# Attention maxima over two PSUM banks at once, and seven of sixteen tiles of the scan's drive by TensorE

## The chip, the core and the metric

The kernel runs on one core of one Trainium2 chip. The metric is the device time of one execution in microseconds; the time of before is the median of three runs. Engines: PE is TensorE, DVE is VectorE, ACT is ScalarE, POOL is GpSimd, SP is the queue that issues the DMAs.

## What is computed

Eight residual steps on x of 2048 tokens by 128 channels: a Mamba block with its own feed-forward, a mixture of experts, causal attention, the experts again, a second Mamba block, a low-rank MLP, causal attention with a position bias, the MLP again. Everything is float32. The change touches the two scans and the two attentions:

```python
# scan, per channel d (256) and state n (16), over the tokens t
h[d,n] = exp(delta[t,d] * A[d,n]) * h[d,n] + delta[t,d] * u[t,d] * B[t,n]
y[t,d] = sum_n h[d,n] * C[t,n]
# attention, 16 heads of 8 channels, 2048 tokens, causal
dots = einsum("hid,hjd->hij", q, k) * scale    (+ bias in the second)
attn = softmax(where(j > i, -max, dots))
out  = einsum("hij,hjd->hid", attn, v)
```

## The kernel before

The kernel is written engine by engine: each engine has its own list of instructions, in the order of the code, and waits on semaphores. Nothing reorders them but the code. Eight stages follow each other.

**The scan** (`mamba_state`, at about 58 to 260 and 1196 to 1400 us of the trace). A step q handles one state number n for 1024 tokens (half k = q // 16 of the tokens), for both halves h = 0, 1 of the channels; there are 32 steps. For each h DVE scans `state = decay * state + drive` over 1024 columns (L596). The two drives, delta\*u\*B, are made in two ways. For h = 0, PE spreads the row of B over the partitions into PSUM (`rows`, L396, two matmuls of 512 columns) and DVE multiplies it by du in place (`make_drive`, L576, 1024 columns). For h = 1, PE makes the first four tiles of 128 tokens as products of the transposed du (`du_T`) with a diagonal of B's column (`products`, L407; the diagonals are made by ACT, L490), POOL multiplies the other 512 columns (`make_part`, L646) and ACT copies them into PSUM (L519). A product of 128 columns stands in the trace as two matmul records. After a scan POOL multiplies the state by C (`read`, L668) and PE adds that up (`sum_states`, L420, eight records of 512 columns a step). PE's order in step q is: rows(q+1), products(q+1), sum_states(q). `products(q)` waits until both scans of step q - 1 are done, `rows(q)` until the first of them is. At the stage's start du is made by four DVE multiplies (`times_u`, L566), the fourth after the first two scans.

**The attention** (`attention`, 524 to 957 and 1505 to 1927 us). For each head there are two passes over the causal half. In the first, PE makes query by key dots into `ps_q` and DVE finds each query's maximum. It goes over 40 *items* a head, numbered n = 0 to 39: an item is one tile t of 128 queries against one chunk kc of 512 keys (`q_items`; t = 0 to 3 have one chunk, t = 12 to 15 have four). An item is a group of four matmuls of 32 columns of the array each (`item`, L1679), which run beside each other. DVE reads its bank in one operation: L1861 for a full chunk, L1858 with the mask for the last one (of 128 to 512 columns, followed by a read of the accumulator). `ps_q` has QB = 3 banks, used in turn; the item that takes use number `use` waits for `bank_free(use)`:

```python
def bank_free(use):
    if use >= QB:
        pe.wait_ge(q_read, use - QB + 1)
```

When a head's 40 maxima are found (L1866), POOL splits them into three bf16 parts, PE turns them (`turn`, L1663, also into a bank of `ps_q`, at position TURN = 5 of the next head's items), DVE casts them (L1849) and SP stores them as three more rows of `q_op`. The second pass makes key by query scores with the maximum already subtracted into `ps_k` (`scores`, L1693, and L1697 for the mask), ACT takes the exp (L1797), and PE multiplies by v (`times_v`, L1715) into `ps_o`, of two banks; ACT copies a finished chunk of 512 queries out (L1805).

PE interleaves both passes. The second pass of a head runs beside the first pass of the next. A *slot* is one scores group and then one item group; after each fourth slot comes one `times_v` of four chunks. Items run LEAD = 14 positions ahead of a head's worth, so the slots of a head's second pass begin with item 14 of the next head, and a `times_v` stands right behind items 1, 5, 9, 13, ... 37:

```python
for a in range(n, n + 4):
    b = NK * h + a
    if b + KB < NK * HEADS:
        scores(b + KB)
    stream(turn, item, NQ + LEAD + b, NQ + LEAD + b + 1)
times_v(h, n)
```

## Time and profile before

| what | us |
|---|---|
| median of 3 runs | 1998.84 |
| lowest, highest | 1994.96, 2001.33 |
| the profiled execution | 1991.66 |
| its span, first to last instruction | 1989.9 |
| PE, DVE, ACT, POOL busy in the span | 1802.1, 1585.1, 1176.7, 592.4 |
| both attentions' second passes (first to last exp) | 400, 399 |
| both scans (first drive to last read) | 201, 201 |

The busy time of an engine is the union of its instructions. For PE it is flattering: the ends of matmuls are modelled, and a group of four overlaps with the next, so starts say more than durations. DVE's and ACT's durations overlap with the next instruction too: what an operation costs its engine is the distance between two starts. "Idle before <-X" names what the engine waited for last.

### The profile page before, as it was taken

The numbers are of one execution on the slowest core, as the hardware profiler recorded it, in microseconds if no ns is written. First come the engines' busy times: TensorE is split into PE (matmuls) and PEld (weight loads), VectorE is DVE, ScalarE is ACT, GpSimd is POOL, SyncE is SP. The second block draws the span as 40 slices with busy tenths as digits, with TensorE's granted clock in tenths as the row PEclk, the third lists the DMA queues.
The fourth block names the chain that finished last, engine by engine and source line by source line (L and its number), as shares of the span: only waits on it lengthen the run. The fifth ranks groups of instructions, "written<-read, shape, count | busy, mean of one in ns | idle before, by whom it ended". The sixth has DMA issues, their size and how long they took to land. (4 is left out here: it accounts for less than half of the span.)

```text
span 1989.9 us, 48041 instructions
## 1 busy us (share of the span) xinstructions
PE 1802.1 (91%) x18610; PEld 961.7 (48%) x18610; DVE 1585.1 (80%) x3424; ACT 1176.7 (59%) x2363; POOL 592.4 (30%) x556
## 2 busy tenths in 40 slices
PE   6888888999799999999899978888888999999988
PEld 2444454444355555555444434444543555555544
DVE  6899966666789999996556678999668999999855
ACT  4676623222268888887422257766352888888855
POOL 3899931000200000004000038999430000000142
PEclk9999998999789999999999998999996999999998
DMA  5433400311312222222041113343012222232200
GB/s 160 121 129 127 128 11 0 86 49 37 106 30 51 51 51 51 51 40 40 1 86 48 37 56 116 133 125 124 1 42 83 49 55 55 56 55 55 31 23 22
DMA packets 68801, 127.94 MB, mean 64 GB/s; under 512 B 20343, under 2 KB 30853, under 8 KB 67165
## 3 DMA queue, kind: packets, MB, share of 16 engines
q1 hardware_dynamic: 68284, 124.34, 24.3%
q8 instruction: 147, 2.41, 0.5%
q14 instruction: 82, 0.66, 0.1%
q10 hardware_dynamic: 288, 0.52, 0.1%
HBM read 107.15 MB, written 16.48 MB: 62 GB/s over the span
## 5 line engine op out<-in xcount | busy, mean ns | idle before, releaser
L1797 ACT ACTIVATE a_probs<-a_ps_k 128x512 f32<-128x512 f32 (+3 forms) x1280 | 599.6, 545 | 216.5 <-PE a_ps_k L1697 135.2
L1861 DVE TENSOR_REDUCE a_maxes<-a_ps_q 128x1 f32<-128x512 f32 x768 | 504.1, 685 | 66.9 <-PE a_ps_q L1679 64.2
L1679 PE MATMUL a_ps_q<-a_k_op,a_q_op 84*32 84x512 bf16 (+7 forms) x5120 | 536.3, 366 | 23.2 <-DMA a_k_op<-a_k_parts 8.7
L1693 PE MATMUL a_ps_k<-a_q_op,a_k_op 87*32 87x512 bf16 (+7 forms) x5120 | 513.0, 351 | 4.0 <-ACT a_probs L1797 3.4
L1715 PE MATMUL a_ps_o<-a_probs,a_vh 128*32 128x512 f32 (+3 forms) x2752 | 316.1, 505 | 0.8 <-ACT a_probs L1797 0.8
L1679 PEld LDWEIGHTS a_ps_q<-a_k_op,a_q_op 72*32 72x32 bf16 (+1 forms) x5120 | 187.1, 97 | 169.7 <-DVE a_maxes L1861 68.8
L1858 DVE CUSTOM_DVE_ANT_0 a_ps_q<-a_ps_q,all_c_mask_q 128x128 f32<-128x128 f32 (+3 forms) x512 | 248.1, 495 | 4.0 <-PE a_ps_q L1679 3.0
L1693 PEld LDWEIGHTS a_ps_k<-a_q_op,a_k_op 75*32 75x32 bf16 (+1 forms) x5120 | 184.1, 96 | 131.7 <-ACT a_probs L1797 78.6
L1113 ACT ACTIVATE e_silu<-e_psg,all_me_b 128x512 f32<-128x512 f32 x128 | 87.7, 687 | 228.1 <-PE e_psg L1045 228.1
L1942 POOL CAST a_max_parts<-a_neg_max 128x16 bf16<-128x16 f32 x32 | 6.3, 196 | 705.3 <-DVE a_neg_max L1866 705.3
L1196 DVE SCALAR_TENSOR_TENSOR e_mid<-e_psv,all_me_b,e_silu 128x512 f32<-128x512 f32 x128 | 95.6, 748 | 129.1 <-PE e_psv L1047 125.2
L172 POOL TENSOR_TENSOR all_rstd<-all_var_eps,all_c_minus_half 128x4 f32<-128x4 f32 x36 | 36.8, 1022 | 467.0 <-DVE all_var_eps L161 466.9
L668 POOL TENSOR_TENSOR m1st_read<-m1st_state,m1st_c_rows 128x1024 f32<-128x1024 f32 x64 | 149.6, 2358 | 11.2 <-PE m1st_psy L420 7.9
L596 DVE TENSOR_TENSOR_SCAN m1st_state<-m1st_decay,m1st_carry,m1st_drive 128x1024 f32<-128x1024 f32 x64 | 146.8, 2334 | 7.6 <-DVE m1st_drive L576 6.4
L668 POOL TENSOR_TENSOR m0st_read<-m0st_state,m0st_c_rows 128x1024 f32<-128x1024 f32 x64 | 149.6, 2359 | 10.7 <-DVE m0st_state L596 6.4
L596 DVE TENSOR_TENSOR_SCAN m0st_state<-m0st_decay,m0st_carry,m0st_drive 128x1024 f32<-128x1024 f32 x64 | 146.8, 2334 | 7.6 <-DVE m0st_drive L576 6.4
L1697 PE MATMUL a_ps_k<-all_c_mask_k,all_c_ident_b 128*32 128x128 bf16 x2048 | 148.5, 221 | 1.1 <-issue 0.9
L1045 PE MATMUL e_psg<-e_xT,all_me_w_T 128*128 128x512 f32 x256 | 133.9, 605 | 1.5 <-ACT e_xT L197 1.5
L1047 PE MATMUL e_psv<-e_xT,all_me_w_T 128*128 128x512 f32 x256 | 132.3, 599 | 0.0
L1034 PE MATMUL e_pso<-e_hid,all_me_w_T 128*128 128x512 f32 x256 | 119.6, 596 | 4.5 <-DVE e_hid L1205 4.5
L1715 PEld LDWEIGHTS a_ps_o<-a_probs,a_vh 128*32 128x32 f32 x2752 | 106.7, 110 | 26.2 <-ACT a_probs L1797 1.1
L420 PE MATMUL m1st_psy<-m1st_read,all_c_ident 128*128 128x512 f32 x256 | 116.1, 594 | 2.0 <-POOL m1st_read L668 1.8
(294 smaller groups left out, 2585.2 us busy)
## 6 DMA issues: line engine op xcount, KB each, us to landing
...
```

The source lines that it names most:

```text
L596: dve.tensor_tensor_scan(state[half(q, h)][:, :], decay[half(q, h)][:, :], drive[:, h, :], carry[:, h, q % NS:q % NS + 1], ALU.mult, ALU.a ...
L668: pool.tensor_tensor(read[h][:, :], state[half(q, h)][:, :], c_rows[q % 2][:, :], ALU.mult).then_inc(read_ready, 1)
L1034: pe.matmul(pso[:, :], w["w3_T"][:, e, f, :], hid[:, k % SL, :], start=k == 0, stop=k == K - 1, skip_group_check=True).then_inc(hid_free, 1)
L1045: pe.matmul(psg[:, f, :], w["w1_T"][:, e, fs], xT[:, tokens(c)], start=True, stop=True).then_inc(g_ready, 1)
L1047: pe.matmul(psv[:, f, :], w["w2_T"][:, e, fs], xT[:, tokens(c)], start=True, stop=True).then_inc(v_ready, 1)
L1679: last = pe.matmul(ps_q[32 * r:32 * r + 32, use % QB, 0:width], q_op[h % SLOT][0:NR, part(t, r)], k_op[h % SLOT][0:NR, kc * CH:kc * CH + w ...
L1693: last = pe.matmul(ps_k[32 * r:32 * r + 32, b % KB, 0:width], k_op[h % SLOT][:, part(j, r)], q_op[h % SLOT][:, c * CH + first:c * CH + fir ...
L1697: last = pe.matmul(ps_k[32 * r:32 * r + 32, b % KB, 0:P], g["ident_b"][:, part(0, r)], g["mask_k"][:, :], start=False, stop=True, skip_gro ...
L1715: pe.matmul(ps_o[rows, c % 2, lo:hi], vh[h % SLOT][:, j, :], probs[:, a % PSLOT, lo - first:hi - first], start=j < 4, stop=j >= TPC * c, s ...
L1797: act.activation(probs[:, n % PSLOT, 0:width], ps_k[:, b % KB, 0:width], ACT.Exp).then_inc(exp_done, 1)
L1858: dve.tensor_tensor_reduce(bank, bank, g["mask_q"][:, CH - width:CH], 1.0, -3e38, ALU.add, ALU.max, found).then_inc(q_read, 1)
L1861: dve.tensor_reduce(found, bank, AX.X, ALU.max).then_inc(q_read, 1)
```

## The change

In the scan, the drive of h = 1 has five tiles made by PE (DIAGONALS = 5) and 384 columns by POOL, and the drive of h = 0 has its first two tiles made by PE (FIRST = 2, `first_products`, with the same diagonals and two more tiles of `du_T`) and 768 columns by DVE. ACT makes five diagonals a step, and its copy into PSUM waits for the fifth tile, which lies in the same bank (`late_made`). Two pieces of the start move: the turn of B's columns stands after four more matmuls on PE, and the fourth `times_u` on DVE before the first scan.

In the attention, the two chunks kc = 0, 1 and the two chunks kc = 2, 3 of a query tile are one *find*: PE fills two neighbouring banks, DVE takes one maximum over up to 1024 columns. There are 24 finds a head, of which 16 take two items: (4, 5), (6, 7), (8, 9), (10, 11), then (12, 13), 14, (15, 16), 17, (18, 19), 20, (21, 22), 23, and (24, 25), (26, 27) and so on to (38, 39). `ps_q` has QB = 2 such double banks, four banks in all, and the bank for that comes from `ps_o`, which has one now. The turn stands at position 6.

```diff
-                for j in range(TPC):
+                for j in reversed(range(DIAGONALS)):
                     last = pe.matmul(drive[:, 1, tile(j)], du_T[:, q // NS, j, :], diag_b[q % 2][:, j, :], start=True, stop=True)
+                    if j == TPC:
+                        last.then_inc(late_made, 1)
...
+            def first_products(q):
+                pe.wait_ge(diag_ready, q + 1)
+                if q % NS == 0:
+                    pe.wait_ge(du_copied, q // NS + 1)
+                if q:
+                    pe.wait_ge(scanned, NH2 * (q - 1) + 1)
+                for j in range(FIRST):
+                    last = pe.matmul(drive[:, 0, tile(j)], du_T[:, q // NS, DIAGONALS + j, :], diag_b[q % 2][:, j, :],
+                                     start=True, stop=True)
+                last.then_inc(first_made, 1)
...
                 if q and q + 1 < STEPS:
+                    first_products(q + 1)
                     rows(q + 1)
                     products(q + 1)
...
-                dve.tensor_tensor(drive[:, 0, :], du[:, 0, time(q)], drive[:, 0, :], ALU.mult).then_inc(drive_ready, 1)
+                dve.tensor_tensor(drive[:, 0, FIRST * P:SCT], du[:, 0, time(q, FIRST * P)], drive[:, 0, FIRST * P:SCT], ALU.mult).then_inc(drive_ready, 1)
...
-        QB = 3
+        QB = 2
         LEAD = 14
-        TURN = 5
+        TURN = 6
...
-        ps_q = m.ps("ps_q", [P, QB, CH])
+        ps_q = m.ps("ps_q", [P, QB, 2 * CH])
-        ps_o = m.ps("ps_o", [P, 2, CH])
+        ps_o = m.ps("ps_o", [P, CH])
...
-                bank_free(use)
+                if n == find_begins[f]:
+                    bank_free(use)
                 for r in range(4):
-                    last = pe.matmul(ps_q[32 * r:32 * r + 32, use % QB, 0:width], q_op[h % SLOT][0:NR, part(t, r)],
+                    last = pe.matmul(ps_q[32 * r:32 * r + 32, use % QB, at:at + width], q_op[h % SLOT][0:NR, part(t, r)],
                                      k_op[h % SLOT][0:NR, kc * CH:kc * CH + width], start=True, stop=True,
                                      skip_group_check=True)
-                last.then_inc(q_ready, 1)
+                if n == find_ends[f]:
+                    last.then_inc(q_ready, 1)
...
-                if n in begins and NC * h + c >= 2:
-                    pe.wait_ge(o_read, NC * h + c - 1)
+                if n in begins and NC * h + c:
+                    pe.wait_ge(o_read, NC * h + c)
...
+                if n != find_ends[f]:
+                    return
+                t, kcs = finds[f]
+                width = min(2 * CH, (t + 1) * P - kcs[0] * CH)
                 dve.wait_ge(q_ready, use + 1)
```

PE's instructions in the first attention from item 19 to item 21, before. Names in brackets are semaphores that the instruction waits for; a semaphore keeps the name of its first holder in the program, and here number 158 is `q_read` and 175 is `exp_done`.

```order
L1679 MATMUL a_ps_q<-a_k_op_274,a_q_op_273 32x512 [waits m0st_summed_158]
L1679 MATMUL a_ps_q<-a_k_op_274,a_q_op_273 32x512 x3
L1693 MATMUL a_ps_k<-a_q_op_271,a_k_op_272 32x384 [waits m0o_t_ready_175]
L1693 MATMUL a_ps_k<-a_q_op_271,a_k_op_272 32x384 x3
L1697 MATMUL a_ps_k<-all_c_mask_k,all_c_ident_b 32x128 x4
L1679 MATMUL a_ps_q<-a_k_op_274,a_q_op_273 32x384 [waits m0st_summed_158]
L1679 MATMUL a_ps_q<-a_k_op_274,a_q_op_273 32x384 x3
L1693 MATMUL a_ps_k<-a_q_op_271,a_k_op_272 32x256 [waits m0o_t_ready_175]
L1693 MATMUL a_ps_k<-a_q_op_271,a_k_op_272 32x256 x3
L1697 MATMUL a_ps_k<-all_c_mask_k,all_c_ident_b 32x128 x4
L1679 MATMUL a_ps_q<-a_k_op_274,a_q_op_273 32x512 [waits m0st_summed_158]
L1679 MATMUL a_ps_q<-a_k_op_274,a_q_op_273 32x512 x3
```

The same place after:

```order
L1715 MATMUL a_ps_q<-a_k_op_276,a_q_op_275 32x512 x4
L1730 MATMUL a_ps_k<-a_q_op_273,a_k_op_274 32x384 [waits m0o_o_read_175]
L1730 MATMUL a_ps_k<-a_q_op_273,a_k_op_274 32x384 x3
L1734 MATMUL a_ps_k<-all_c_mask_k,all_c_ident_b 32x128 x4
L1715 MATMUL a_ps_q<-a_k_op_276,a_q_op_275 32x384 [waits m0st_carried_158]
L1715 MATMUL a_ps_q<-a_k_op_276,a_q_op_275 32x384 x3
L1730 MATMUL a_ps_k<-a_q_op_273,a_k_op_274 32x256 [waits m0o_o_read_175]
L1730 MATMUL a_ps_k<-a_q_op_273,a_k_op_274 32x256 x3
L1734 MATMUL a_ps_k<-all_c_mask_k,all_c_ident_b 32x128 x4
L1715 MATMUL a_ps_q<-a_k_op_276,a_q_op_275 32x512 [waits m0st_carried_158]
L1715 MATMUL a_ps_q<-a_k_op_276,a_q_op_275 32x512 x3
```

Items 19, 20 and 21 and the scores between them stand in the same order; item 19 no longer waits, and item 21's wait is now for the double bank of items 18 and 19.

PE in the scan, one step, before (m0st_read is summed up, then the next step's rows and products):

```order
L407 MATMUL m0st_drive<-m0st_diag_b_106,m_du_T 128x128 x4
L420 MATMUL m0st_psy<-m0st_read_100,all_c_ident 128x512 x2
L420 MATMUL m0st_psy<-m0st_read_101,all_c_ident 128x512 x2
L396 MATMUL m0st_drive<-m_bc_82,all_c_sel 128x512 x2
L407 MATMUL m0st_drive<-m0st_diag_b_107,m_du_T 128x128 x4
```

and after:

```order
L440 MATMUL m0st_psy<-m0st_read_100,all_c_ident 128x512 x2
L440 MATMUL m0st_psy<-m0st_read_101,all_c_ident 128x512 x2
L417 MATMUL m0st_drive<-m0st_diag_b_107,m_du_T 128x128 x2
L406 MATMUL m0st_drive<-m_bc_82,all_c_sel 128x256
L406 MATMUL m0st_drive<-m_bc_82,all_c_sel 128x512
L425 MATMUL m0st_drive<-m0st_diag_b_107,m_du_T 128x128 x5
L440 MATMUL m0st_psy<-m0st_read_100,all_c_ident 128x512 x2
```

Two products now stand ahead of the rows, and the rows that DVE waits for are behind them.

DVE at the first stage's start, from around the copy of B's columns to behind the first two scans, before:

```order
L607 COPY m_b_cols<-m0stin_turned 128x320
L566 TENSOR_TENSOR m_du<-m_delta,m_u 128x2x512 x2
L570 COPY m_du_T<-m0stin_acc 128x512
L576 TENSOR_TENSOR m0st_drive<-m_du,m0st_drive 128x1024
L566 TENSOR_TENSOR m_du<-m_delta,m_u 128x2x512
L596 SCALAR_TENSOR_TENSOR m0st_state_105<-m0st_decay_98,m0st_carry,m0st_drive 128x1024
L596 SCALAR_TENSOR_TENSOR m0st_state_102<-m0st_decay_99,m0st_carry,m0st_drive 128x1024
L570 COPY m_du_T<-m0stin_acc 128x512
L566 TENSOR_TENSOR m_du<-m_delta,m_u 128x2x512
```

and after:

```order
L592 TENSOR_TENSOR m_du<-m_delta,m_u 128x2x512
L636 COPY m_b_cols<-m0stin_turned 128x400
L592 TENSOR_TENSOR m_du<-m_delta,m_u 128x2x512
L597 COPY m_du_T<-m0stin_acc 128x896
L604 TENSOR_TENSOR m0st_drive<-m_du,m0st_drive 128x768
L592 TENSOR_TENSOR m_du<-m_delta,m_u 128x2x512 x2
L624 SCALAR_TENSOR_TENSOR m0st_state_105<-m0st_decay_98,m0st_carry,m0st_drive 128x1024
L624 SCALAR_TENSOR_TENSOR m0st_state_102<-m0st_decay_99,m0st_carry,m0st_drive 128x1024
L597 COPY m_du_T<-m0stin_acc 128x896
```

The fourth multiply into m_du has moved ahead of both scans, and the copies of du_T are 896 columns wide.

## Rows read from the trace of the kernel before

**Rows 1.** Busy time by stretches of 80 us (scan) and 300 us (attention): us, engines, PEclk
```profile
75.00:155.00 80.00, 67.47 (x246) 34.46 (x247) 77.18 (x42) 56.81 (x124) 79.96 (x42) 1.00 0.38 129
...
600.00:900.00 300.00, 296.87 (x5820) 173.87 (x5818) 275.61 (x717) 248.34 (x541) 13.47 (x65) 1.00 0.27 49
```

**Rows 2.** Timeline of DVE in the attention: start us, us, engine, line, operation
```profile
676.43 0.14 DVE L1858 DVE_READ_ACCUMULATOR2_ANT a_maxes<- 128x1 f32 x1
...
677.03 0.27 DVE L1849 CAST a_max_T<-a_ps_q 48x128 bf16<-48x128 f32 x1
...
678.22 0.69 DVE L1861 TENSOR_REDUCE a_maxes<-a_ps_q 128x1 f32<-128x512 f32 x1 [0.65 <-PE a_ps_q L1679]
...
701.43 0.27 DVE L1849 CAST a_max_T<-a_ps_q 48x128 bf16<-48x128 f32 x1
```

**Rows 3.** Timeline of PE, same stretch: turn of the maxima, items around it
```profile
672.95 0.41 PE L1679 MATMUL a_ps_q<-a_k_op,a_q_op 72*32 72x512 bf16 x4
...
673.70 0.29 PE L1679 MATMUL a_ps_q<-a_k_op,a_q_op 72*32 72x256 bf16 x4
...
676.16 0.24 PE L1663 MATMUL a_ps_q<-all_c_ident_b,a_max_parts 128*32 128x128 bf16 x2
...
676.63 0.24 PE L1679 MATMUL a_ps_q<-a_k_op,a_q_op 72*32 72x128 bf16 x4 [0.23 <-DVE a_maxes L1858]
...
677.77 0.39 PE L1679 MATMUL a_ps_q<-a_k_op,a_q_op 72*32 72x512 bf16 x4
...
680.35 0.39 PE L1693 MATMUL a_ps_k<-a_q_op,a_k_op 75*32 75x512 bf16 x4
```

**Rows 4.** Timeline of PE, one head earlier: items 13 to 24
```profile
657.07 0.39 PE L1679 MATMUL a_ps_q<-a_k_op,a_q_op 72*32 72x512 bf16 x4
...
658.17 0.54 PE L1679 MATMUL a_ps_q<-a_k_op,a_q_op 72*32 72x512 bf16 x4
...
660.73 0.38 PE L1679 MATMUL a_ps_q<-a_k_op,a_q_op 72*32 72x512 bf16 x1
...
661.58 0.40 PE L1679 MATMUL a_ps_q<-a_k_op,a_q_op 72*32 72x512 bf16 x3
...
662.79 0.39 PE L1679 MATMUL a_ps_q<-a_k_op,a_q_op 72*32 72x512 bf16 x3
...
663.66 0.45 PE L1679 MATMUL a_ps_q<-a_k_op,a_q_op 72*32 72x512 bf16 x4
```

**Rows 5.** Timeline of DVE in the attention: maxima back to back
```profile
706.19 1.28 DVE L1861 TENSOR_REDUCE a_maxes<-a_ps_q 128x1 f32<-128x512 f32 x2
...
707.39 0.29 DVE L1858 CUSTOM_DVE_ANT_0 a_ps_q<-a_ps_q,all_c_mask_q 128x128 f32<-128x128 f32 x1
...
707.60 1.28 DVE L1861 TENSOR_REDUCE a_maxes<-a_ps_q 128x1 f32<-128x512 f32 x2
```

**Rows 6.** Timeline of the scan, one step: DVE, then PE
```profile
185.93 1.20 DVE L576 TENSOR_TENSOR m0st_drive<-m_du,m0st_drive 128x1024 f32<-128x1024 f32 x1
...
187.34 4.58 DVE L596 TENSOR_TENSOR_SCAN m0st_state<-m0st_decay,m0st_carry,m0st_drive 128x1024 f32<-128x1024 f32 x2 [0.20 <-DVE m0st_drive L576]
...
191.84 1.21 DVE L576 TENSOR_TENSOR m0st_drive<-m_du,m0st_drive 128x1024 f32<-128x1024 f32 x1
...
186.16 1.13 PE L407 MATMUL m0st_drive<-m0st_diag_b,m_du_T 128*128 128x128 f32 x8 [0.91 <-DVE m0st_state L596]
...
187.13 3.60 PE L420 MATMUL m0st_psy<-m0st_read,all_c_ident 128*128 128x512 f32 x8
...
190.56 0.60 PE L396 MATMUL m0st_drive<-m_bc,all_c_sel 96*128 96x512 bf16 x2
```

**Rows 7.** DMA issues: operands, count, size, us to landing
```profile
a_q_parts<-a0pr_q_parts SPq DMA_DIRECT2D x12, 128.0 KB, 2.5
```

**Rows 8.** Groups by line: ACT's copy of the outputs
```profile
L1805 ACT ACTIVATE a_o_sb<-a_ps_o 128x512 f32<-128x512 f32 x128 | 75.9, 593 | 2.2 <-PE a_ps_o L1715 2.2
```

**Rows 9.** Timeline of DVE at the first scan's start
```profile
66.68 3.02 DVE L566 TENSOR_TENSOR m_du<-m_delta,m_u 128x1024 f32<-128x1024 f32 x1
```

More of the change, by code:

```diff
@@ L41 @@
 NSC = TOK // SCT
+DIAGONALS = 5
+FIRST = 2
+MADE = DIAGONALS * P
+LATE = SCT - MADE
 FF = 512
@@ L250, in mamba_state @@
         state.insert(0, m.sb("state0", [P, SCT]))
-        diag_b = [m.sb(f"diag_b{s}", [P, TPC, P]) for s in range(2)]
+        diag_b = [m.sb(f"diag_b{s}", [P, DIAGONALS, P]) for s in range(2)]
         carry = m.sb("carry", [P, NH2, NS])
@@ L333, in early_chunk @@
             return k * SCT // CH
+        turned_tiles = [(1, j) for j in range(DIAGONALS)] + [(0, j) for j in range(FIRST)]
         def time(q, first=0, last=SCT):
@@ L347, in turn_b @@
                 for k in range(NSC):
[L348 to L350 removed]
+                    pe.wait_ge(xd_ready, early_chunk(k) + 2)
+                    for j in range(DIAGONALS):
+                        at = (DIAGONALS * k + j) * XDBL
                         last = pe.transpose(turned[:, 1, at:at + XDBL], xd[0:XDBL, tile(TPC * early_chunk(k) + j)], g["ident"][0:XDBL, 0:XDBL])
@@ L395, in rows @@
                 for b in range(NB):
-                    last = pe.matmul(drive[:, 0, chunk(b)], g["sel"][:, q % NS, :], bc3[:, time(q, b * CH, (b + 1) * CH)],
+                    lo, hi = max(b * CH, FIRST * P), (b + 1) * CH
+                    last = pe.matmul(drive[:, 0, lo:hi], g["sel"][:, q % NS, :], bc3[:, time(q, lo, hi)],
                                      start=True, stop=True)
                 last.then_inc(rows_spread, 1)
-            def products(q):
+            def first_products(q):
                 pe.wait_ge(diag_ready, q + 1)
@@ L488, in diagonals @@
                     act.wait_ge(product_ready, q - 1)
-                for j in range(TPC):
+                for j in range(DIAGONALS):
                     last = act.activation(diag_b[q % 2][:, j, :], g["ident"][:, :], ACT.Identity,
@@ L516, in _ @@
                 act.wait_ge(part_ready, q + 1)
+                act.wait_ge(late_made, q + 1)
+                if q == 0:
+                    act.wait_ge(du_copied, 1)
                 if q:
                     act.wait_ge(scanned, NH2 * q)
-                act.activation(drive[:, 1, MADE:SCT], part[q % 2][:, :], ACT.Copy).then_inc(part_placed, 1)
+                act.activation(drive[:, 1, MADE:SCT], part[q % 2][:, 0:LATE], ACT.Copy).then_inc(part_placed, 1)
                 carry_over(q - 1, 1)
@@ L614, in _ @@
             times_u(2)
+            times_u(3)
             scans(0)
             copy_turned(1)
-            times_u(3)
             for q in range(1, STEPS):
@@ L645, in make_part @@
                     pool.wait_ge(part_placed, q - 1)
-                pool.tensor_tensor(part[q % 2][:, :], du[:, 1, time(q, MADE)], b_rows[q % 2][:, :],
+                pool.tensor_tensor(part[q % 2][:, 0:LATE], du[:, 1, time(q, MADE)], b_rows[q % 2][:, 0:LATE],
                                    ALU.mult).then_inc(part_ready, 1)
@@ L1588, in attention @@
         NQ = len(q_items)
+        finds = [(t, tuple(kc for kc in range(t // TPC + 1) if kc // 2 == half)) for t in range(NT) for half in range(t // TPC // 2 + 1)]
+        find_of = [f for f, (t, kcs) in enumerate(finds) for kc in kcs]
+        find_begins = [find_of.index(f) for f in range(len(finds))]
+        find_ends = [b - 1 for b in find_begins[1:]] + [NQ - 1]
         q_begins = [min(i for i, (t, kc) in enumerate(q_items) if t // TPC == c) for c in range(NC)]
@@ L1712, in times_v @@
                     if c == 0 and j:
-                        pe.matmul(ps_o[rows, 0, 0:first], zeros[:, :], g["sel"][:, 0:j, :], start=True, stop=True,
+                        pe.matmul(ps_o[rows, 0:first], zeros[:, :], g["sel"][:, 0:j, :], start=True, stop=True,
                                   skip_group_check=True)
-                    pe.matmul(ps_o[rows, c % 2, lo:hi], vh[h % SLOT][:, j, :], probs[:, a % PSLOT, lo - first:hi - first],
+                    pe.matmul(ps_o[rows, lo:hi], vh[h % SLOT][:, j, :], probs[:, a % PSLOT, lo - first:hi - first],
                               start=j < 4, stop=j >= TPC * c, skip_group_check=True).then_inc(pv_done, 1)
```

103 lines of the change are left out of this document (56 added, 47 removed).

## Prediction

> **What bounds the kernel now.** I read the busy table by stretches first. In the attentions PE is busy 296.9 of 300 us, DVE 275.6, ACT 248.3, at full clock; in the scan POOL is busy 80.0 of 80 us, DVE 77.2, PE 67.5 [rows 1]. The two casts of the maxima one head apart, 677.03 and 701.43, give the attention's beat, 24.40 us a head [rows 2]. Then the timeline of PE alone: item groups (four 32-column matmuls of 512 columns) and scores groups follow each other every 0.22 us: from item 22 at 662.79 to item 24 at 663.66 stand four of them in 0.87 us [rows 4], and 512 columns at 2.4 GHz are 0.213. So PE streams nearly without a gap, and whatever stops it is added to the head. The one long stop is at the turning of the maxima: turn at 676.16, next item at 676.63, 0.47 us for a group worth 0.06, "idle 0.23 <-DVE" [rows 3]. By the starts below DVE has maxima for 21 us of the 24.4, and waits for PE in between. **PE is the bound of the attentions, DVE is not, though it is close.**
>
> In the scan DVE sets the step: drive at 185.93, scans at 187.34, next drive at 191.84, so 5.91 us, with no wait but 0.20 us for its own result. PE ends its last rows matmuls (190.56 + 0.60) at 191.16, 0.68 us before DVE wants them [rows 6].
>
> **The attention's part.** It removes 16 of 40 DVE operations a head. From starts, a 512-column maximum costs 0.60 us (two from 706.19 to 707.39) and a 128-column one 0.21 (707.39 to 707.60) [rows 5], so 0.13 us for each 128 columns and some 0.07 fixed: DVE saves 16 x 0.07 = 1.1 us a head, worth nothing while PE is the bound. What is left is the buffering. Before, an item group needed the bank of three uses ago; now a group that begins a find needs the double bank of two finds ago, and both groups of that find must have been read in one operation. That takes, from the start of the find's last group: 0.45 us until DVE starts (group 677.77, DVE 678.22 [rows 2, 3]); 0.69 us for a 512-column maximum [rows 5] plus 512 more columns at 1.04 ns, together 1.22; and 0.06 us until PE's next matmul (the read of the accumulator ends at 676.57, PE starts 676.63 [rows 2, 3]). **1.73 us.** Each beginning find has that only if the eight products with v (0.86 us) stand between, since two slots (a scores and an item group each) without them are 0.87 us [rows 4]. Going through the 24 finds of a head in the order of the code with LEAD = 14, where a product block follows items 1, 5, 9, ... 37:
> - Item 1 needs find (38, 39). 672.95 to 673.70 is 0.75 [rows 3]: stop 0.98.
> - Item 4 needs item 2's bank, of 384 columns: the groups between them are 1920 columns, 0.82 us at 0.22 for 512; the read needs 0.39 + 0.61 + 0.06 = 1.06: 0.24.
> - Item 15 needs find (12, 13). 657.07 to 658.17 is 1.10 [rows 4]: 0.63, plus up to 0.3 as DVE still reads the 1024 columns before it, whose two slots gave it 0.87 for 1.14. I take 0.8.
> - Item 18 needs find (15, 16): a product block of uneven pieces stands between, 0 to 0.5. I take 0.1, since item 15's stop has already spread them.
> - Item 21 needs find (18, 19). The last group of 19 starts at 660.73, item 21 at 661.58, 0.85: 0.88.
> - Item 24 needs find (21, 22). 662.79 to 663.66, 0.87: 0.86 to 0.93; I take 0.9.
> - All others have a product block or a short find between them: no stop.
>
> Sum 3.9 us. The stop at the turn, 0.41, goes: the turn now stands behind a product block. But it comes a slot and a block later: the distance from it to the next head's first scores, 676.16 to 680.35, 4.2 us, shrinks to 2.6 (from 677.77 [rows 3]), and the maxima need about 0.3 to DVE, 0.27 for the cast [rows 2], and 2.5 to land (the nearest is the landing of the q parts, larger but to the same side [rows 7]): 3.1, a stop of 0.5, between 0 and 1; I take 0.3. Net 3.9 - 0.4 + 0.3 = **3.8 us a head**, 28.2 for 24.4. It applies to items 54 to 640 of each attention, 14.65 heads, 29.3 in both: **+110 us**. Bounds: half of the stops hidden in PE's short queues gives 2.8 a head, +82; every bound at its top, 4.7, +138. The first head, items alone, I put at nothing (DVE bound, 1.1 less, against a refill that now waits longer). Removing an output buffer (ps_o) puts times_v of a new chunk behind ACT's copy of the last one, 0.59 us, before which ACT waited for PE 2.2 us in 128 copies [rows 8]. The copy follows the exp that the block waits for anyway, so PE can be stopped 0 to 0.5 us four times a head; since PE, stopped by the finds, will be behind ACT, I take 0.
>
> DVE shows the stop's other side: the 1024 columns cost it a fixed 0.07 less. The Trainium skill, Perfetto Trace Analysis, section Optimizing Scalar/DVE Operations, says both that grouping into larger operations helps "if the engine is saturated", and that where Vector is not saturated but causes bubbles elsewhere, breaking instructions up lets work complete sooner. By the first DVE would be the bound and the change gain; by the second it loses. Rows 1 and 3 put this kernel in the second case.
>
> **The scan's part.** DVE's drive goes from 1024 to 768 columns, 256 x 1.04 ns = 0.27 us less a step; POOL's part from 512 to 384, a quarter of a job that is 1.28 with its fixed cost, so about as much. The step would be 5.64. PE pays: three more products at 0.243 (four took 186.16 to 187.13) less 256 columns of rows, 0.11 [rows 6]. Its chain from the end of the scans: products at +0.23 after the drive's start, then 5 x 0.243 + 3.43 (187.13 to 190.56) + 2 x 0.243 + 0.11 + 0.38 and 0.04 to DVE = 5.88. In a step where the scans end first PE is late by 0.24; in the next PE had no wait and only 5.65 is asked. The two alternate: 5.76, **0.15 us less a step**, 29 steps, two stages: -9. Bounds: 0.03 and 0.27 a step, -2 and -16. At the start of each stage DVE's fourth times_u took 3.02 us [rows 9] where the same 1024 columns of drive take 1.20: it ran beside POOL's read. It moves ahead of the first scan, where POOL waits: up to 1.8 gained, against wider copies (three tiles, 0.4 us each) and a fifth diagonal: I take -1 a stage, 1 either way. **-11 in all.** In a sentence apart: the Trainium skill, SBUF — State Buffer, section Who interferes with whom, says a tensor_tensor with both inputs in SBUF contends with GpSimd's reads; the 3.02 us agree.
>
> **Sum.** 1991.7 (profiled run, 1989.9 of it span) + 110 - 11 = 2091. The median shown, 1998.8, is 7.2 above the profiled run, so **2098**.
>
> **Rivals.**
> - *As meant: no stop.* PE's queues and DVE's lead cover the reuse. Then the turn's 0.41 goes, 29.3 x 0.4 = 12 us, and the scan's 11: 1999 - 23 = 1976. For it: DVE gets 1.1 us a head more room. Against: it decides at 1.73 us between a find's last group and its reuse, and four places give 0.75 to 1.1. If DVE were the bound after all, 1.1 x 29.3 = 32 more, 1944. Chance 0.10 together.
> - *Half of it.* The stops overlap with waits that PE has anyway (ACT's, the turn's): 1.5 to 2.5 a head, 2035 to 2060. For it: a stopped PE meets ACT further ahead, so that the short waits it has for ACT now go. Chance 0.08.
> - *More than it.* The single output buffer stops PE 0.3 us four times a head, 35 us more, or the clock falls. Against the clock: the scan keeps 1.00 with PE busy 84% [rows 1], and the attention would be at 85%. 2133 to 2170, chance 0.08.
> - *The scan alone differs*: -2 to -18, inside the range. That it gains nothing and the attention too: within 0.3%, 0.02.
>
> **How the numbers follow.** The forecast has 0.72, from 2062 (2.8 a head, scan -18) to 2135 (4.7 a head, scan -2). The range 2040 to 2140 takes in most of the half case and the low end of the one with more, and leaves out 0.19. Faster by over 0.3% (about what a measurement of this kernel can tell from no change) 0.10, within 0.02, slower 0.88.
>
> **What would show it.** In the profile after: the casts of the maxima about 28.2 us apart instead of 24.40; PE's idle before items naming DVE, near 1 us each, at items 1, 15, 21 and 24; busy PE some 85% in the attention; maxima over 1024 columns at 1.14 us from start to start (were it 1.5, every stop grows by 0.35). In the scan, steps of 5.64 and 5.88 in turn, and DVE's drive waiting for PE's rows. Wrong if the casts stay within 25 us of each other: then the reuse distance is not what the groups' starts say.

## The result

| | before | after |
|---|---|---|
| median, us | 1996.9 (1994.77 to 2001.33) | 2117.32 (2114.72 to 2120.89) |
| ratio | 1 | 1.0597, 95% interval 1.0573 to 1.0621 |
| profiled execution, its span | 1991.66, 1989.9 | 2114.72, 2112.9 |

The kernel became 6% slower. The forecast was 2098, in a range of 2040 to 2140; the loss is 120 us where 99 were forecast. The gap between the two profiled spans, 123.0 us, divides as follows. The times are differences between rows of the traces: a scan stage from the end of its last copy into xd to its last read, a first head from the first item to the first exp, the later heads from the first exp to the last.

| stretch, us | before | after | difference | forecast |
|---|---|---|---|---|
| scans | 208.3, 209.1 | 210.1, 210.1 | +2.8 | -11 |
| first heads of the attentions | 32.1, 32.0 | 37.4, 36.8 | +10.1 | 0 |
| other heads | 400.4, 399.7 | 454.0, 455.0 | +108.9 | +110 |
| the rest | 708.2 | 709.5 | +1.3 | 0 |

(The last column was worked out ahead of the result for other stretches' ends, so it is right to about 1 us.)

**The attention's heads.** The casts of the maxima, on DVE after the change:

```profile
701.04 0.28 DVE L1886 CAST a_max_T<-a_ps_q 48x128 bf16<-48x128 f32 x1 [0.23 <-PE a_ps_q L1696]
...
729.23 0.28 DVE L1886 CAST a_max_T<-a_ps_q 48x128 bf16<-48x128 f32 x1 [0.23 <-PE a_ps_q L1696]
...
757.44 0.28 DVE L1886 CAST a_max_T<-a_ps_q 48x128 bf16<-48x128 f32 x1 [0.23 <-PE a_ps_q L1696]
```

They stand 28.19 and 28.21 us apart, where it was 24.40 [rows 2]. PE over one head after the change; the columns are start, us, engine, line, operation, tiles, and in brackets the idle time before it with what ended it:

```profile
677.63 0.40 PE L1730 MATMUL a_ps_k<-a_q_op,a_k_op 75*32 75x512 bf16 x4
678.63 0.40 PE L1715 MATMUL a_ps_q<-a_k_op,a_q_op 72*32 72x512 bf16 x4 [0.60 <-DVE a_maxes L1901]
...
682.02 0.23 PE L1734 MATMUL a_ps_k<-all_c_mask_k,all_c_ident_b 128*32 128x128 bf16 x4
683.02 0.40 PE L1715 MATMUL a_ps_q<-a_k_op,a_q_op 72*32 72x512 bf16 x4 [0.77 <-DVE a_maxes L1901]
...
684.88 0.39 PE L1730 MATMUL a_ps_k<-a_q_op,a_k_op 75*32 75x512 bf16 x4
685.95 0.40 PE L1715 MATMUL a_ps_q<-a_k_op,a_q_op 72*32 72x512 bf16 x4 [0.68 <-DVE a_maxes L1901]
...
695.63 0.40 PE L1730 MATMUL a_ps_k<-a_q_op,a_k_op 75*32 75x512 bf16 x4
696.92 0.29 PE L1715 MATMUL a_ps_q<-a_k_op,a_q_op 72*32 72x256 bf16 x4 [0.89 <-DVE a_maxes L1898]
...
698.72 0.41 PE L1730 MATMUL a_ps_k<-a_q_op,a_k_op 75*32 75x512 bf16 x4
699.20 0.40 PE L1715 MATMUL a_ps_q<-a_k_op,a_q_op 72*32 72x512 bf16 x4
...
700.78 0.22 PE L1696 MATMUL a_ps_q<-all_c_ident_b,a_max_parts 128*32 128x128 bf16 x2
700.87 0.40 PE L1715 MATMUL a_ps_q<-a_k_op,a_q_op 72*32 72x512 bf16 x4
...
703.24 0.39 PE L1715 MATMUL a_ps_q<-a_k_op,a_q_op 72*32 72x512 bf16 x4
703.65 0.40 PE L1730 MATMUL a_ps_k<-a_q_op,a_k_op 75*32 75x512 bf16 x4
```

These are the stops of the prediction, in its places. The group after a 512-column group should start 0.22 us later. Item 15 starts 1.00 after its predecessor (677.63 to 678.63), so it stops 0.78; item 21 stands 1.00 behind a mask group worth 0.06, a stop of 0.94; item 24 1.07 behind a group worth 0.22, so 0.85; item 1 (256 columns, 696.92) 1.29, so 1.07; item 4 (699.20) 0.48 behind a group worth 0.22, so 0.26, though no bracket stands there. The turn at 700.78 is followed by an item at 700.87: its stop is gone. The first scores of the next head, at 703.65, come 0.41 behind an item of 512 columns: 0.19 for the landing of the maxima.

There is a sixth stop, at item 18, which the prediction gave 0.1. No bracket shows it, since PE still had pieces of the product block at work. PE at items 16 to 19 and DVE's read of items 15 and 16, after the change:

```profile
679.07 0.39 PE L1715 MATMUL a_ps_q<-a_k_op,a_q_op 72*32 72x512 bf16 x4
...
679.51 0.28 PE L1715 MATMUL a_ps_q<-a_k_op,a_q_op 72*32 72x256 bf16 x4
...
680.79 0.40 PE L1715 MATMUL a_ps_q<-a_k_op,a_q_op 72*32 72x512 bf16 x4
...
681.30 0.39 PE L1715 MATMUL a_ps_q<-a_k_op,a_q_op 72*32 72x512 bf16 x4
```

```profile
679.51 1.23 DVE L1901 TENSOR_REDUCE a_maxes<-a_ps_q 128x1 f32<-128x1024 f32 x1 [0.68 <-PE a_ps_q L1715]
```

and items 17 and 19 before:

```profile
659.19 0.29 PE L1679 MATMUL a_ps_q<-a_k_op,a_q_op 72*32 72x256 bf16 x4
...
660.49 0.38 PE L1679 MATMUL a_ps_q<-a_k_op,a_q_op 72*32 72x512 bf16 x1
```

Item 18 starts at 680.79, 1.72 us after item 16's group (679.07) and 0.05 after the end of the read (679.51 + 1.23 = 680.74): the same chain as in the other places. From item 17 to item 19 it is 1.79 us where it was 1.30, so 0.49 more. Item 21, in turn, had stood late before the change too: from item 19 to item 21 it is 1.72 us where it was 1.09 (660.49 to 661.58 [rows 4]), 0.63 more and not 0.94. With 0.49 at item 18 and 0.63 at item 21, and 1.07, 0.26, 0.78 and 0.85 in the other places, 0.19 for the landing and 0.41 less at the turn, the head is 3.86 us longer by this count; 3.79 were measured.

DVE shows the price of one long read:

```profile
684.67 1.22 DVE L1901 TENSOR_REDUCE a_maxes<-a_ps_q 128x1 f32<-128x1024 f32 x1 [1.17 <-PE a_ps_q L1715]
685.81 0.69 DVE L1898 CUSTOM_DVE_ANT_0 a_ps_q<-a_ps_q,all_c_mask_q 128x512 f32<-128x512 f32 x1
```

From 684.67 to 685.81, 1.14 us for 1024 columns, as in the prediction's working. DVE did save its 16 operations, and stands idle for them: over the same 300 us as in [rows 1] the row is

```profile
600.00:900.00 300.00, 268.01 (x5060) 135.31 (x5056) 238.26 (x450) 220.99 (x470) 11.41 (x55) 1.00 0.24 43
```

PE is busy 268.0 us of 300 where it was 296.9, DVE 238.3 where it was 275.6. The clock is 1.00 in this stretch in both kernels, with PE idle for 0.60 to 0.89 us four times in each 28 us after the change. Nothing of the loss in these heads is clock.

**The scan.** DVE and then PE in two steps after the change:

```profile
188.48 0.96 DVE L604 TENSOR_TENSOR m0st_drive<-m_du,m0st_drive 128x768 f32<-128x768 f32 x1
...
194.14 0.94 DVE L604 TENSOR_TENSOR m0st_drive<-m_du,m0st_drive 128x768 f32<-128x768 f32 x1
...
199.98 0.96 DVE L604 TENSOR_TENSOR m0st_drive<-m_du,m0st_drive 128x768 f32<-128x768 f32 x1
...
188.43 1.38 PE L425 MATMUL m0st_drive<-m0st_diag_b,m_du_T 128*128 128x128 f32 x10
...
193.53 0.49 PE L406 MATMUL m0st_drive<-m_bc,all_c_sel 96*128 96x256 bf16 x2
194.29 1.38 PE L425 MATMUL m0st_drive<-m0st_diag_b,m_du_T 128*128 128x128 f32 x10 [0.27 <-DVE m0st_state L624]
```

The drives start at 188.48, 194.14 and 199.98: steps of 5.66 and 5.84 in turn, where it was 5.91 [rows 6]. The mean is 0.16 less. Yet the stage gains nothing, because its opening costs more. PE and ACT at the first drive, after the change:

```profile
56.10 1.28 ACT L523 ACT_TABLE_LOAD   x1
57.40 1.15 ACT L523 ACTIVATE m0st_decay<-m_delta,m_neg_a 128x1024 f32<-128x1024 f32 x1
58.45 1.55 ACT L513 ACTIVATE m0st_diag_b<-all_c_ident,m_b_cols 128x128 f32<-128x128 f32 x5
...
60.06 1.23 PE L417 MATMUL m0st_drive<-m0st_diag_b,m_du_T 128*128 128x128 f32 x4 [3.46 <-ACT m0st_diag_b L513]
...
69.29 2.50 PE L425 MATMUL m0st_drive<-m0st_diag_b,m_du_T 128*128 128x128 f32 x10 [0.31 <-DVE m0st_state L624]
```

The first drive (DVE, 61.52) waits for the two products of `first_products`, these for ACT's diagonals, and ACT makes those only after loading its table and the first decay. From the end of the last copy into xd to the first drive it is 11.75 us where it was 6.76. TensorE's clock falls 8 to 10 us after that copy in both kernels. After the change it stays at 0.50 for 13.5 us; before, it did for 3.3 us in the first scan and for 10.1 in the second. The rows, after and then before, have the stretch, its length, the busy us and records of PE, of its weight loads, of DVE, ACT and POOL, the granted clock, the DMA share and GB/s:

```profile
59.50:73.00 13.50, 10.66 (x39) 8.50 (x40) 11.35 (x8) 8.63 (x20) 5.65 (x3) 0.50 0.02 5
```

```profile
61.50:64.80 3.30, 3.27 (x14) 2.81 (x14) 2.27 (x2) 3.30 (x7) 2.09 (x2) 0.50 0.11 29
1198.10:1208.20 10.10, 7.40 (x25) 5.42 (x26) 9.07 (x6) 9.37 (x21) 7.31 (x4) 0.50 0.10 33
```

At 0.50 TensorE runs at its lower level, 1.2 GHz: the ten product records took 2.50 us at 69.29, and 1.38 at 188.43. The scan of before varies along with this: its second to third drive takes 5.85 us in the first scan and 6.97 in the second, and over the six kernels that keep this scan (before, att_alone, one_output_bank, four_banks, reads_apart, lead_15) a stage takes 208.1 to 210.1 us, 209.4 in the mean. So the +2.8 of the table is exact for the two traces only; against the mean it is +1.4. Both are far from the -11 that was forecast.

### The profile page after: what moved, and what is told of

Same layout as the page of the kernel before. It is cut to its first block and busy times, and to the rows that moved or that the text cites. A ratio compares the mean times of both kernels' runs of the same rounds, so it can differ in the third digit from the quotient of the medians.

```text
span 2112.9 us, 48465 instructions
## 1 busy us (share of the span) xinstructions
PE 1874.9 (89%) x19010; PEld 970.0 (46%) x19010; DVE 1563.6 (74%) x2912; ACT 1197.1 (57%) x2427; POOL 572.9 (27%) x556
## 5 line engine op out<-in xcount | busy, mean ns | idle before, releaser
L1834 ACT ACTIVATE a_probs<-a_ps_k 128x512 f32<-128x512 f32 (+3 forms) x1280 | 611.7, 539 | 321.7 <-PE a_ps_k L1734 202.1
L1715 PE MATMUL a_ps_q<-a_k_op,a_q_op 84*32 84x512 bf16 (+7 forms) x5120 | 500.5, 368 | 115.5 <-DVE a_maxes L1901 73.3
L1730 PE MATMUL a_ps_k<-a_q_op,a_k_op 87*32 87x512 bf16 (+7 forms) x5120 | 500.6, 352 | 4.0 <-ACT a_probs L1834 2.3
L1898 DVE CUSTOM_DVE_ANT_0 a_ps_q<-a_ps_q,all_c_mask_q 128x128 f32<-128x128 f32 (+7 forms) x512 | 385.8, 769 | 91.6 <-PE a_ps_q L1715 82.0
L1901 DVE TENSOR_REDUCE a_maxes<-a_ps_q 128x1 f32<-128x1024 f32 x256 | 313.0, 1223 | 93.5 <-PE a_ps_q L1715 93.2
L1715 PEld LDWEIGHTS a_ps_q<-a_k_op,a_q_op 72*32 72x32 bf16 (+1 forms) x5120 | 151.3, 98 | 304.8 <-DVE a_maxes L1901 127.4
L1730 PEld LDWEIGHTS a_ps_k<-a_q_op,a_k_op 75*32 75x32 bf16 (+1 forms) x5120 | 166.1, 96 | 123.8 <-ACT a_probs L1834 63.1
L176 POOL TENSOR_TENSOR all_rstd<-all_var_eps,all_c_minus_half 128x4 f32<-128x4 f32 x36 | 36.8, 1023 | 469.9 <-DVE all_var_eps L165 469.8
L696 POOL TENSOR_TENSOR m0st_read<-m0st_state,m0st_c_rows 128x1024 f32<-128x1024 f32 x64 | 149.5, 2357 | 21.9 <-DVE m0st_state L624 12.4
L1734 PE MATMUL a_ps_k<-all_c_mask_k,all_c_ident_b 128*32 128x128 bf16 x2048 | 128.2, 221 | 0.0
L1752 PEld LDWEIGHTS a_ps_o<-a_probs,a_vh 128*32 128x32 f32 x2752 | 98.3, 110 | 53.0 <-ACT a_o_sb L1842 12.6
```

The lines of the kernel that those rows point to most:

```text
L696: pool.tensor_tensor(read[h][:, :], state[half(q, h)][:, :], c_rows[q % 2][:, :], ALU.mult).then_inc(read_ready, 1)
L1715: last = pe.matmul(ps_q[32 * r:32 * r + 32, use % QB, at:at + width], q_op[h % SLOT][0:NR, part(t, r)], k_op[h % SLOT][0:NR, kc * CH:kc * ...
L1730: last = pe.matmul(ps_k[32 * r:32 * r + 32, b % KB, 0:width], k_op[h % SLOT][:, part(j, r)], q_op[h % SLOT][:, c * CH + first:c * CH + fir ...
L1734: last = pe.matmul(ps_k[32 * r:32 * r + 32, b % KB, 0:P], g["ident_b"][:, part(0, r)], g["mask_k"][:, :], start=False, stop=True, skip_gro ...
L1752: pe.matmul(ps_o[rows, lo:hi], vh[h % SLOT][:, j, :], probs[:, a % PSLOT, lo - first:hi - first], start=j < 4, stop=j >= TPC * c, skip_gro ...
L1834: act.activation(probs[:, n % PSLOT, 0:width], ps_k[:, b % KB, 0:width], ACT.Exp).then_inc(exp_done, 1)
```

## The experiments

All are timed against the kernel before on the same chip. reads_apart, lead_15, five_alone and first_alone were run once each, so there is a trace and a single time for them.

### att_alone: the attention's change on the scan of before

Against the kernel after, all of the scan's change is undone:

```diff
-DIAGONALS = 5
-FIRST = 2
...
                 if q and q + 1 < STEPS:
-                    first_products(q + 1)
                     rows(q + 1)
```

> The attention's change alone, on the scan of before. My theory (PE waits for a double bank to be read, 3.8 us a head): casts of the maxima 28.2 us apart, first head of each attention 4 to 5 longer too, so 110 + 9 = 119 us more than before, within 3 of the whole change. Rival (the scan's part carries some of the loss, since the scan's 31 steps in all show none of the 11 us forecast): 105 to 112 more than before.

Measured: 2116.56 against 1997.47, ratio 1.0594 (1.0565 to 1.0623). Casts 28.2 apart, first heads 37.6 and 37.2 us, the other heads 454.2 and 455.2. The attention carries the whole loss, +119; the rival falls.

### one_output_bank: before, with one bank less for ps_o

```diff
-        ps_o = m.ps("ps_o", [P, 2, CH])
+        ps_o = m.ps("ps_o", [P, CH])
...
-                if n in begins and NC * h + c >= 2:
-                    pe.wait_ge(o_read, NC * h + c - 1)
+                if n in begins and NC * h + c:
+                    pe.wait_ge(o_read, NC * h + c)
```

> Before, with one bank for the output of the second pass (ps_o) instead of two; one bank of PSUM stays unused. My theory, in which ACT's copy of the output stops PE for nothing: casts still 24.4 apart, within 3 us of before. Rival (part of the 3.8 us a head is the single output bank): up to 4 x 0.3 us a head, 35 us more.

Measured: 2001.01 against 1997.47, ratio 1.0013 (0.9988 to 1.0037), no difference that can be measured. The trace has it finer: most casts are 24.46 apart, 0.06 a head more than before, which is 2 us in all. Single heads take up to 1.7 us more in this trace (26.07, 25.57 and 25.55), as one does in the trace of before (25.51). With them the later heads of both attentions are 8.2 us longer in this trace; the interval of the times ends at 7.4 us more. So the bank that was taken from the output costs between nothing and some 8 us, and the rival's 35 fall.

### four_banks: the same banks, not paired

Against the kernel before, with one_output_bank's edit of `times_v` besides:

```diff
-        QB = 3
+        QB = 4
         LEAD = 14
         TURN = 5
...
-        ps_q = m.ps("ps_q", [P, QB, CH])
         with ExitStack() as early:
             turned = Memory(nc, early, tag + "pr").ps("turned", [P, 2, CH])
-        ps_o = m.ps("ps_o", [P, 2, CH])
+        ps_q = m.ps("ps_q", [P, QB, CH])
+        ps_o = m.ps("ps_o", [P, CH])
```

> The same four banks for the maxima and one for the output as after the change, but each item has a bank of its own, read and released alone, as before (QB = 4, TURN = 5). My theory: the bank was not the cost, the pairing was. No stop at items 1, 15, 21, 24, and the turn's 0.41 us stop goes too, since the item behind it has a spare bank: casts 23.9 to 24.0 apart, 12 to 16 us less than before. Rival (the order, the output bank or the turn costs): 26 or more.

Measured: 1986.98 against 1997.47, ratio 0.9946 (0.9930 to 0.9962): 10.5 us less, a little short of the 12 to 16 that were expected. Casts of its DVE:

```profile
703.63 0.27 DVE L1849 CAST a_max_T<-a_ps_q 48x128 bf16<-48x128 f32 x1
727.65 0.27 DVE L1849 CAST a_max_T<-a_ps_q 48x128 bf16<-48x128 f32 x1
```

24.02 us, 0.38 less than before: the turn's stop of 0.41 is gone, and nothing has come. PE's items as a group, in the page's form (line, engine, operation, tiles and count, busy us and mean ns, idle us before them with what ended it), in this kernel, before and after the change:

```profile
L1679 PE MATMUL a_ps_q<-a_k_op,a_q_op 84*32 84x512 bf16 (+7 forms) x5120 | 551.4, 365 | 15.4 <-DMA a_k_op<-a_k_parts 10.9 <-issue 1.6 <-DVE a_maxes L1858 1.3
```

```profile
L1679 PE MATMUL a_ps_q<-a_k_op,a_q_op 84*32 84x512 bf16 (+7 forms) x5120 | 536.3, 366 | 23.2 <-DMA a_k_op<-a_k_parts 8.7 <-DVE a_maxes L1858 8.4 <-DVE a_maxes L1861 3.2
```

```profile
L1715 PE MATMUL a_ps_q<-a_k_op,a_q_op 84*32 84x512 bf16 (+7 forms) x5120 | 500.5, 368 | 115.5 <-DVE a_maxes L1901 73.3 <-DVE a_maxes L1898 33.3 <-DMA a_k_op<-a_k_parts 6.2
```

With four single banks PE's idle time before items that is put down to DVE is 1.3 us for the masked reads and less than that for the others, in both attentions together (8.4 and 3.2 with three banks); with the same four banks read and released in pairs it is 73.3 and 33.3 us. The loss is the pairing's.

### reads_apart: double banks, read half by half

Against att_alone:

```diff
-                if n == find_ends[f]:
-                    last.then_inc(q_ready, 1)
+                last.then_inc(q_ready, 1)
...
-                if n != find_ends[f]:
-                    return
...
-                width = min(2 * CH, (t + 1) * P - kcs[0] * CH)
+                width = min(CH, (t + 1) * P - kc * CH)
```

(A double bank is released by the count of its second half; `bank_free` waits for that.)

> Double banks as after the change, released as a pair, but DVE reads each half as soon as its group is in: from the last group to the release only 0.45 + 0.69 + 0.06 = 1.20 us instead of 1.73. My theory: stops of about 0.45 (item 1), 0.24 (item 4), 0.1 to 0.3 (item 15), 0.35 (item 21) and 0.33 (item 24), the turn as after: casts 25.4 to 26.2 apart, although DVE has the 16 operations back. Rival (the length of the chain does not matter, only the number of double banks): 28.2.

Measured: 2058.77 in one run, casts 26.3 apart (719.27 and 745.58), 1.9 more than before and 1.9 less than after. The stops follow the length of the chain, 0.53 us shorter. It is a little more than the upper end expected. Two of its stops on PE:

```profile
794.00 0.29 PE L1691 MATMUL a_ps_q<-a_k_op,a_q_op 72*32 72x256 bf16 x4 [0.53 <-DVE a_maxes L1872]
...
807.27 0.40 PE L1691 MATMUL a_ps_q<-a_k_op,a_q_op 72*32 72x512 bf16 x4 [0.35 <-DVE a_maxes L1875]
```

The one at 794.00 is item 1, 0.53 by the bracket where it was 0.89, the one at 807.27 item 21, 0.35 where it was 0.77: 0.36 and 0.42 less, not the whole 0.53. At item 21 DVE's row shows why: it reads the two halves in one row, and the second can't start before the first is done.

```profile
805.93 1.29 DVE L1875 TENSOR_REDUCE a_maxes<-a_ps_q 128x1 f32<-128x512 f32 x2 [0.38 <-PE a_ps_q L1691]
```

It ends at 807.22, and item 21 starts 0.05 later: 1.55 us after item 19's group (805.72 in the trace) and not 1.20.

### lead_15: the product blocks one item later

Against att_alone:

```diff
-        LEAD = 14
+        LEAD = 15
```

> att_alone with LEAD = 15, so that the product blocks stand behind items 2, 6, 10, ... 38 and not 1, 5, 9, ... 37. My theory (a stop is 1.73 us less what stands between a double bank's last group and its reuse): the count over the finds gives stops at items 1, 2, 6, 10, 14, 15, 18, 21, 34 and 38, some 5.3 us for 4.2, and none for the landing of the maxima: casts 28.9 to 29.6 apart. Rival (the stop does not depend on where the blocks stand): 28.2, or less by the landing that is gone.

Measured: 2158.68 in one run, casts 29.68 apart, 1.5 more than in att_alone and just above the range. One number, that changes no work at all, costs 42 us: it puts product blocks where the finds don't need them. Six of its stops in a head have a bracket; these are the three at items 38, 6 and 14, that have no stop with LEAD = 14 (the others are 1, 18 and 21; all six are on the list of what was expected):

```profile
700.93 0.40 PE L1687 MATMUL a_ps_q<-a_k_op,a_q_op 72*32 72x512 bf16 x4 [0.17 <-DVE a_maxes L1870]
...
707.78 0.40 PE L1687 MATMUL a_ps_q<-a_k_op,a_q_op 72*32 72x512 bf16 x4 [0.52 <-DVE a_maxes L1870]
...
713.49 0.24 PE L1687 MATMUL a_ps_q<-a_k_op,a_q_op 72*32 72x128 bf16 x4 [0.29 <-DVE a_maxes L1870]
```

### scan_alone: the scan's change on the attention of before

Against the kernel after, all of the attention's change is undone:

```diff
-        QB = 2
+        QB = 3
...
-                if n == find_ends[f]:
-                    last.then_inc(q_ready, 1)
+                last.then_inc(q_ready, 1)
```

> The scan's change alone, on the attention of before. The trace of the whole change has steps of 5.66 and 5.83 us in turn (before 5.91), but from the last chunk's copy (xd) to the last drive of a stage it needs 1.0 and 1.8 us more than before. My theory: the opening of each stage loses 5 to 6 us (the first drive waits for ACT's diagonals, TensorE's clock stays at 0.50 from 60 to 72 us), the steps give 4.4 back: 0 to 3 us more than before. Rival (the opening differs only by run, my forecast of -11 holds): 8 to 14 less.

Measured: 1996.55 against 1997.5, ratio 1.0009 (0.9991 to 1.0028): no difference. The forecast of 11 us less falls. In the trace the stages take 210.1 and 209.9 us, the steps are 5.66 and 5.83 in turn, and from the last copy to the third drive it is 30.4 us against 24.0 and 25.2 before.

### five_alone and first_alone: one half of the scan's change each

Against scan_alone:

```diff
-FIRST = 2
+FIRST = 0
```

```diff
-DIAGONALS = 5
+DIAGONALS = 4
```

> scan_alone without the two tiles of h = 0 (FIRST = 0, DIAGONALS = 5): DVE's drive has all 1024 columns again. My theory: DVE sets the step at 5.90 to 5.91 as before, POOL gets idle. Rival (POOL set the step before): 5.6 to 5.75. The opening is that of before, since the first drive needs no diagonals.

> scan_alone with four tiles of h = 1 (FIRST = 2, DIAGONALS = 4): DVE has 768 columns, POOL again 512. POOL's two reads and its part are 2 x 2.31 + 1.28 = 5.90. My theory: POOL takes over as the bound, steps of 5.88 to 5.92. Rival (DVE alone set the step): 5.64 to 5.76. The opening is that of scan_alone.

Measured, one run each: five_alone 1990.07, steps 5.91; first_alone 1996.93, steps mostly 5.85 to 5.87, just below what was expected. Neither half gives more than some 0.05 us a step, both together 0.16. Before, DVE and POOL both filled the step, and each half relieves only one of them: in the steps of five_alone POOL waits 0.28 us for DVE and DVE has no gap but its own 0.20, in those of first_alone POOL has none. five_alone's first drive comes 7.4 us after the last copy, those of first_alone 11.2 and 11.3: it is the tiles of h = 0 that tie the first drive to the diagonals. (The single times are not read: the stretches outside scans and attentions alone differ from run to run by several us, 704.6 in five_alone, 709.3 in first_alone, 715.4 in one_output_bank.)

### scan_diagonals_first: ACT's order at the opening

Against scan_alone:

```diff
             for q in range(STEPS):
-                exps(q, 0)
                 if q == 0:
                     act.wait_ge(b_copied, 1)
                     diagonals(0)
+                exps(q, 0)
                 exps(q, 1)
```

> scan_alone, with ACT making the first step's diagonals ahead of its table load and first decay. My theory (the first drive waits for the diagonals): first drive some 2.5 us earlier, and PE's idle ahead of it shorter; each stage 2.5 to 4 us shorter than in scan_alone, so 3 to 8 us less than before in all. Rival (the opening hangs on something else, say on the copies or POOL): the same as scan_alone.

Measured: 1989.56 against 1997.5, ratio 0.9971 (0.9954 to 0.9988), and 7 us less than scan_alone on the same chip. First drive 9.0 us after the last copy (11.75 in scan_alone), stages 207.3 and 206.3. All as expected. The wait for ACT's diagonals is shown as the first cause, with 2.7 of the 5.0 us. The rest isn't ACT's order: in this trace the copy of the turned du starts 6.9 us after the last copy into xd (6.2 before), is 0.4 us longer, and the first drive waits another 1.06 for `first_products`, which stand behind it:

```profile
59.74 0.68 PE L417 MATMUL m0st_drive<-m0st_diag_b,m_du_T 128*128 128x128 f32 x4 [1.27 <-DVE m_du_T L597]
```

### scan_skip_early: work in PE's gap

Against scan_diagonals_first:

```diff
             turn_du(0)
+            pe.wait_ge(delta_ready, NH2 * NC)
+            pe.wait_ge(b_copied, 1)
+            skip(0, 1)
             first_products(0)
...
-            pe.wait_ge(delta_ready, NH2 * NC)
             pe.wait_ge(du_copied, 2)
-            skip(0)
+            skip(0, 0)
```

> scan_diagonals_first, with half of the skip products (u times D, four matmuls of 512 columns for h = 1) ahead of the first products, where PE stands idle. My theory (a part of the opening is TensorE's clock, at 0.50 from about 65 to 72 us, and PE's chain of products, skip and sum, which POOL's second step waits for): the clock stays at 1.00 longer, 1.7 us of the chain go, the stretch from the second to the third drive falls from 10.0 and 9.2 towards 6 to 8: each stage 2 to 4 us shorter than in scan_diagonals_first. Rival (the chain is not PE's): the same as scan_diagonals_first.

Measured: 1990.31 against 1997.0, ratio 0.9974 (0.9953 to 0.9994). By the medians it is no better than scan_diagonals_first, by its trace it is: stages 205.1 and 204.9, from the second drive to the third 7.6 us in both (10.0 and 9.2 there). 2.2 and 1.4 us a stage is less than these medians tell apart. TensorE's low stretch, by the same columns as above, in this kernel and in scan_diagonals_first (it is at 1.00 for some us right before and after):

```profile
62.20:69.00 6.80, 5.82 (x23) 4.69 (x24) 6.67 (x6) 4.48 (x11) 4.44 (x2) 0.50 0.00 0
```

```profile
65.20:72.00 6.80, 5.40 (x18) 4.08 (x19) 6.67 (x5) 4.69 (x11) 5.63 (x3) 0.50 0.04 7
```

The clock is at 0.50 for 6.8 us in both, so the move did not keep it up, against what was expected. The last copy into xd ends 1.9 us earlier in this kernel's trace (49.8 for 51.6); counted from there the clock falls at 12.4 us where it fell at 13.6, and is back 1.1 us sooner. In the second scan it is back no sooner, and the stretch is shorter by 1.6 us all the same. So most of the gain is the four matmuls that left the chain, about 1.7 us; how much of the first scan's 2.4 us is the clock isn't measured apart.

### both_better: four_banks and scan_skip_early

> scan_skip_early with the attention of four_banks. My theory: the gains add, 10.5 from the four banks and what scan_skip_early has against before (some 12): 1970 to 1980. Rival (they meet in the same waits): no better than the better of the two.

The edits of both, and nothing else. Measured: 1981.09 (1973.99 to 1989.67) against 1997.0, ratio 0.9923 (0.9895 to 0.9950): some 16 us faster than before and 136 faster than after. The upper end of what was expected is missed by 1 us, since scan_skip_early had turned out to be worth 7 us and not the 12 in that sum; 10.5 and 6.7 are 17.2. Its trace has heads of 24.02 and stages of 205.1 and 204.8: the gains add.

## Why the prediction was right, and where it was off

- **PE is the bound of the attentions, DVE is not.** Right. DVE's saving became idle time (238.3 busy of 300; PE 268.0, which is 89%, where some 85 were forecast), and reads_apart, which gives DVE its operations back, is 58 us faster than att_alone. The Trainium skill, Perfetto Trace Analysis, section Optimizing Scalar/DVE Operations, has both rules, and its second one, for an engine that is not saturated but causes bubbles elsewhere, is the one that holds here, with DVE busy 275.6 of 300 us before: att_alone is the grouping, +119 us, and four_banks the same banks in the smaller pieces, -10.5.
- **1.73 us from a find's last group to its reuse, against what stands between.** Right as a chain and in four places: 0.98, 0.24, 0.8 and 0.9 were forecast for items 1, 4, 15 and 24, and 1.07, 0.26, 0.78 and 0.85 measured. Items 18 and 21 were sized wrong, with 0.1 and 0.88 for 0.49 and 0.63. The reason given for the 0.1, that item 15's stop spreads them, does not hold: item 18 waits the full 1.72 us from item 16's group. That the two errors nearly cancel in the sum is luck. reads_apart shortens the chain and lead_15 changes what stands between, and the stops follow both.
- **The turn: 0.4 gained, 0.3 lost in landing.** Right in kind; the landing's stop is 0.19.
- **The output bank at nothing.** Right to within some 8 us: 0.06 a head in most heads of one_output_bank, and no difference that its times can tell.
- **Net 3.8 us a head, +110.** 3.79 and +108.9.
- **The first head at nothing.** Wrong: +5.3 and +4.8. The step called it bound by DVE, with 1.1 us less to do, and named the longer refill without a price. Before, it was bound by DVE, with TensorE at 0.50; after, it no longer is (the same columns of busy time, before and after):

```profile
530.00:548.00 18.00, 16.72 (x140) 3.71 (x132) 17.98 (x45) 0.00 (x0) 0.00 (x0) 0.50 0.40 125
```

```profile
530.00:548.00 18.00, 12.02 (x112) 2.60 (x112) 13.61 (x24) 0.00 (x0) 0.00 (x0) 0.50 0.41 126
```

DVE was busy 17.98 of 18 us and is now 13.61. The same chain holds there, with no scores and no products in between at all (PE after the change):

```profile
539.02 1.37 PE L1715 MATMUL a_ps_q<-a_k_op,a_q_op 72*32 72x512 bf16 x12 [1.11 <-DVE a_maxes L1901]
541.39 1.47 PE L1715 MATMUL a_ps_q<-a_k_op,a_q_op 72*32 72x512 bf16 x12 [1.01 <-DVE a_maxes L1901]
```

Two finds of a query tile take 2.37 us (539.02, 541.39), and each time PE has waited about 1 us for a read of 1024 columns. The working that was made for the later heads had the chain, and was not applied to the head where nothing covers it.
- **The scan's step, -0.15.** Right: 5.66 and 5.84 for 5.64 and 5.88, every second step longer because of PE. From the third drive to the last read the two stages together are 8.7 us shorter, where -9 was forecast for the steps.
- **The opening, -1 a stage.** Wrong: +6.4 and +5.0 us from the last copy to the third drive (30.5 and 30.2 for 24.0 and 25.2). The part that was priced, the fourth `times_u`, did give back: from the first drive to the second it is 8.62 us where it was 11.43. What was not priced is that `first_products` makes DVE's first drive wait for ACT's diagonals, behind a table load and a decay: +4.99 us to the first drive. Nor was it priced that the clock stays at the lower level for 13.5 us, which with the chain of products, skip and sums makes the stretch from the second drive to the third 10.1 and 9.8 us; in the twelve stages of the six kernels with the scan of before it is 5.85 to 7.53. The wait for the diagonals (2.7 us) and the skip matmuls in the chain (1.6 us in a stage) are shown by experiments; the clock's own share is not. The added wait was followed through the steps, and not through the first one.
- **The size.** Later heads 1 less, first heads 10 more, scans 14 more than forecast, the rest 1: 2091 was forecast for the profiled run, and 2115 came. Of the medians, 2098 was forecast and 2117 came, the median of before being 2 us lower in this comparison. The bounds "-2 to -18" for the scan did not hold the scan's +2.8; the range of the sum held because the heads' bounds were wide; both large misses went the same way, so that it held has some luck in it.

The rival "more than it" (2133 to 2170) missed the time by 16 us, where the forecast missed it by 19, for reasons that are refuted: neither the output bank nor the clock in the attention.
